# Moving the second batch's layer norm from cycles 1 to 5 into cycles 4 and 5 of the first batch's attention

## The reference

```python
x = L0_attn_x                                   # (8, 512, 256) float32
x = x + attn(_layernorm(x), gamma, w_qkv, w_out)
x = x + ffn(_layernorm(x), router_w, w1, b1, w2, b2)

def _layernorm(x, axis=-1, eps=1e-05):
    m = jnp.mean(x, axis=axis, keepdims=True)
    v = jnp.var(x, axis=axis, keepdims=True)
    return (x - m) / jnp.sqrt(v + eps)

xn = rms_norm(x, gamma); qkv = xn @ w_qkv       # inside attn
sim = einsum('bhid,bhjd->bhij', q * 64 ** -0.5, k)
out = einsum('bhij,bhjd->bhid', softmax(sim), v)  @ w_out
```

## Time and profile before

| | |
|---|---|
| median of 3 runs | 1148.58 us |
| lowest, highest | 1147.79, 1149.24 us |
| the profiled execution | 1149.06 us, of which its span is 1147.3 us |
| TensorE busy | 1132.5 us (99%) |
| VectorE busy | 1010.4 us (88%) |
| ScalarE busy | 859.6 us (75%) |
| GpSimd busy | 671.2 us (59%) |

### The profile page before, as it was taken

One profiled execution on the slowest core, in us unless ns is written; L12 is line 12 of the kernel. 1 busy time (PEld: TensorE's weight loads), 2 busy tenths in 40 slices (PEclk: granted clock), 3 DMA queues, 4 the chain that ended last, 5 costly groups with the idle time before them and its releaser, 6 DMA issues.

```text
span 1147.3 us, 29822 instructions
## 1 busy us (share of the span) xinstructions
PE 1132.5 (99%) x11664; PEld 959.6 (84%) x11664; DVE 1010.4 (88%) x1768; ACT 859.6 (75%) x1899; POOL 671.2 (59%) x827
## 2 busy tenths in 40 slices
PE   8999999999999999999999999999999999999998
PEld 6778888888888888888888888888888877888887
DVE  6899899889988998999898988898989988989975
ACT  6878888888888888888888888888888885334432
POOL 6776656565656565656565666666656576223421
PEclk9999999999999999999999999999999999999999
DMA  4134112311231123212221222122312235335321
GB/s 124 51 88 112 39 38 75 93 39 38 75 93 38 39 75 85 46 39 74 63 70 38 66 61 66 35 74 57 75 39 56 75 94 152 131 118 150 105 76 38
DMA packets 58284, 83.15 MB, mean 72 GB/s; under 512 B 12576, under 2 KB 34592, under 8 KB 58144
## 3 DMA queue, kind: packets, MB, share of 16 engines
q1 hardware_dynamic: 58144, 81.24, 26.1%
HBM read 31.14 MB, written 16.25 MB: 41 GB/s over the span
## 4 chain that ended last, share of the span: by engine, by line
PE 88%; DVE 8%; ACT 1%; issue 1%; POOL 1%; DMA 0%; SPq 0%; ACTq 0%; DVEq 0%; POOLq 0%
PE ps L659 22%; PE ps L777 19%; PE ps L809 14%; PE ps L697 10%; PE ps L742 10%; PE ps L703 5%; PE ps L952 3%; DVE pT_lo L1398 3%; PE ps L956 2%; DVE negmax L1485 1%; DVE f_o L1675 1%; PE ps L755 1%; ACT prob L1114 1%; DVE xT_lo L1399 1%; PE ps L957 1%
## 5 line engine op out<-in xcount | busy, mean ns | idle before, releaser
L1245 POOL TENSOR_SCALAR prob<-prob,rowinv 128x512 f32<-128x512 f32 x512 | 358.4, 716 | 323.6 <-DVE rowinv L1490 321.7
L1114 ACT ACTIVATE prob<-ps,negmax 128x512 f32<-128x512 f32 x512 | 349.2, 696 | 75.4 <-DVE negmax L1485 75.4
L1485 DVE TENSOR_REDUCE negmax<-ps 128x2 f32<-128x1024 f32 x256 | 311.6, 1218 | 56.5 <-PE ps L703 56.1
L1398 DVE TENSOR_TENSOR pT_lo<-ps,pT_hi 128x512 fp32r<-128x512 f32 (+1 forms) x384 | 319.0, 858 | 35.0 <-ACT pT_hi L1107 20.8
L742 PEld LDWEIGHTS ps<-identity,prob 64*128 64x128 f32 x4096 | 167.0, 139 | 40.0 <-DVE pT_lo L1398 5.9
L742 PE MATMUL ps<-identity,prob 64*128 64x64 f32 x4096 | 169.1, 222 | 2.8 <-DVE pT_lo L1398 2.0
L697 PE MATMUL ps<-nat 64*128 64x512 f32 x1024 | 166.1, 402 | 4.3 <-DVE nat L1398 2.4
L809 PE MATMUL ps<-xT_hi,wbig 64*128 64x512 f32 x992 | 159.1, 398 | 0.0
L1104 ACT ACTIVATE pT_hi<-ps 128x1024 fp32r<-128x1024 f32 x128 | 131.5, 1028 | 32.3 <-issue 23.7
L777 PE MATMUL ps<-pT_hi,vbuf 64*128 64x512 f32 x992 | 145.4, 411 | 0.0
L1107 ACT ACTIVATE pT_hi<-ps 128x512 fp32r<-128x512 f32 x256 | 140.2, 608 | 0.6 <-PE ps L742 0.5
(11 more groups left out here) (118 smaller groups left out, 2008.4 us busy)
## 6 DMA issues: line engine op xcount, KB each, us to landing
att_hi_v<-halves_out SPq DMA_DIRECT2D x128, 128.0 KB, 2.3
att_lo_v<-halves_out SPq DMA_DIRECT2D x128, 128.0 KB, 2.4
blocks_scratch<-xblocks SPq DMA_DIRECT2D x15, 512.0 KB, 3.0
xn<-blocks_scratch SPq DMA_DIRECT2D x60, 128.0 KB, 2.8
xin<-in_x SPq DMA_DIRECT2D x32, 128.0 KB, 3.2
xres<-in_x SPq DMA_DIRECT2D x8, 512.0 KB, 3.5
x_scratch<-xres SPq DMA_DIRECT2D x8, 512.0 KB, 2.6
xin<-x_scratch SPq DMA_DIRECT2D x32, 128.0 KB, 3.3
```

Source lines behind the costliest of these rows:

```text
L1114: act.activation(prob[:, n % NPROB, j * SEQ:(j + 1) * SEQ], ps[:, score_banks(n) + j, :], ACT.Exp, bias=negmax[:, n % 4, j:j + 1], accum_o ...
L1245: return pool.tensor_scalar(dst, src, scalar, 1.0, ALU.mult, ALU.mult)
L1398: return dve.tensor_tensor(dst, full, hi, ALU.subtract)
L1485: dve.tensor_reduce(negmax[:, n % 4, :], ps[:, score_banks(n):score_banks(n) + 2, :], AX.X, ALU.max, negate=True).then_inc(s_max, 1)
```

## The change

For the first batch alone another table is used. The four statistics steps stand in slots 16 to 19, which is cycle 4 (two in each half of the cycle), the normalisation of four tiles in slots 20 and 21 and the two block transposes in slots 22 and 23, which is cycle 5. Step 10 is left out for this batch, where it did nothing. The other batches keep their table.

```diff
 LN_SLOTS = {5: 0, 7: 1, 9: 2, 11: 3, 13: 10, 15: 6, 17: 8, 19: 9, 21: 13}
+FIRST_LN_SLOTS = {16: 0, 17: 1, 18: 2, 19: 3, 20: 6, 21: 8, 22: 9, 23: 13}
 LAST_LN_SLOT = NUNIT
...
             b, rel = divmod(slot, SPB)
-            return (b + 1, LN_SLOTS[rel]) if rel in LN_SLOTS and 0 <= b < B else None
+            places = LN_SLOTS if b else FIRST_LN_SLOTS
+            return (b + 1, places[rel]) if rel in places and 0 <= b < B else None
```

## The result

The changed kernel takes 1151.72 us (median of 8 runs, 1150.81 to 1153.53); eight runs of the kernel before have a median of 1149.11 us. The ratio is 1.0026, 95% interval 1.0017 to 1.0034: slower by about 0.26%, beyond what the measurement leaves open. (A ratio is worked out from all the runs of both kernels, so it can lie a few hundredths of a per cent off that of the two medians, here 1.0023.) The forecast was 1150.1 us and no change that can be told; it is wrong in both. The median lies 0.02 us above the top of the forecast's range. The profiled execution took 1150.88 us with a span of 1149.1, +1.8 us on that of before.

The account below looks back on a forecast made before the run. TensorE, busy 99% of the span, was taken to bound the kernel. -0.52 - 1.03 + 3.05 = +1.50 us on the profiled 1149.06 gave 1150.6, or 1150.1 on the median's scale; range 1147.7 to 1151.7.

Parts of the forecast that it names:

- Cycles 1 to 3: Statistics steps and normalisations removed from these cycles shorten them by 0.52 us together, bounds -0.3 and -0.75.
- Cycle 4: Normalisations leave, statistics come in; both TensorE waits go and the cycle becomes 14.95 us, -1.03.
- rival 3: Cycle 4: statistics are blocked too, beside GpSimd's split of chunk 6; +2.9 in sum, 1151.5 us; chance 0.06.
- the 1.30 us of the second half's steps: Cycle 4, ahead of tile 18's row maximum: two statistics, the aggregation and the variance take 1.30 us.
- Cycle 5: Four normalisations meet GpSimd's split of chunk 7; one stands until the split's low part ends; the cycle loses 3.05 us.
- rival 1: Cycle 5: normalisations run back to back and GpSimd's split is held up; -0.70 in sum, 1147.9 us; chance 0.12.
- rival 4: Cycle 5 has room for the moved steps and keeps its length; -1.55 in sum, 1147.0 us; chance 0.05.
- a stall at part speed: Cycle 5: VectorE and GpSimd share the port at part speed; four normalisations take 4.3 us, kernel near 1150.8.
- the wait for the exponential: Cycle 5: TensorE waits 0.7 us for an exponential, besides some 2 us for the low part of tile 18.
- rival 2: Cycle 5: TensorE's clock falls to 1.2 GHz behind its 2.0 us pause, costing 3.06 us; chance 0.07.
- The anchor: Base of the sum: profiled 1149.06 us lies 0.48 above the three-run median 1148.58, so 1150.6 becomes 1150.1.

Follow-up runs that it names:

- Experiment 2: Changed kernel with GpSimd's split of weight chunk 7 moved four slots later, from cycle 5 to cycle 6: 1148.43 us, ratio 0.9992.
- the second measurement: The changed kernel run again without an edit: 1151.65 us (11 runs), ratio 1.0024 against the kernel before.
- experiment 3: Changed kernel with 14 unneeded matmuls ahead of the queries and keys of pair 6, filling TensorE's pause in cycle 5: 1152.05 us, ratio 1.0026.
- filled kernels: 14 unneeded matmuls added to the changed kernel in cycle 5 (1152.05 us), or to the kernel before in cycle 5 (1151.65) or cycle 16 (1150.45).
- experiment 7: Changed kernel with another first-batch table, first normalisations in slot 15, the others in slot 19: 1147.97 us; with first two statistics in slots 7 and 8, 1147.99.
- 8-step kernels: Kernel before with 8 extra statistics steps in each of four cycles (1157.87 us), or in cycle 16 alone with a 192-byte (1152.96) or 1024-byte buffer (1151.37).

## Why the prediction was wrong

- **Cycles 1 to 3**: right, -0.58 for -0.52.
- **Cycle 4**: right in its mechanism, -0.89 for -1.03. Both waits went, the statistics were not blocked (rival 3 falls). The mis-sized term is the 1.30 us of the second half's steps: they took 1.47, because the variance, a small tensor-by-scalar instruction, took 0.39 us. The forecast had used cycle 2, where it took 0.19 and had begun in the same moment as GpSimd's multiplication (45.42). In cycle 4 it began 0.33 us into one and ended with it.
- **Cycle 5**: right, +3.03 for +3.05, with the place, the instruction that stands (2562 ns) and the instruction that makes it stand. GpSimd was not held up (rival 1 falls), there was no room (rival 4 falls), and a stall at part speed would have put the low part at +6.3, where it came at +5.57. Experiment 2 shows GpSimd's split as the cause. That the wait for the exponential was 0.48 us and not 0.7 cost nothing in the sum, which did not use it.
- **The step that failed is rival 2, TensorE's clock, which the sum had at nothing.** I saw the 2.0 us pause, gave the fall 0.07 and left it out of the range, with the words "no pause in this trace brought it about; none was that long". That the trace held no such pause was a lack of evidence, and I counted it as evidence against. The runs showed a lower clock in 15 of 19 executions of the changed kernel, and in none of 81 of before or of 11 with the pause gone (experiment 2). It cost 1.3 us where a profile caught it. The 3.06 of the rival was too much: a stretch of 3.4 us at half the clock can cost at most its half, 1.7 us, and the block behind the pause took 1.48 more, not its own length once more. As a term of the sum the clock is 15/19 x 1.3 = +1.0 by this estimate: 1.56 + 1.0 = +2.6. The medians gave +2.61 and, in the second measurement, +2.30; the ratios +3.0 and +2.8.
- **The anchor.** I took off 0.48 us to come from the profiled execution to the median of three runs. The kernel before measured 1149.11, 1149.35, 1149.32, 1148.45 and 1149.64 in the sets of runs since: that median had been a low one, and the 1149.06 of the profiled execution was the better base. Of the 1.62 us between forecast and result (1151.72 - 1150.1) this makes 0.53, the clock about 1.0 and the cycles 0.06. With the clock and without this step the sum gives 1149.06 + 2.6 = 1151.7.
- **Chance in it.** The result lies 0.02 us outside the range; the second measurement, 1151.65, would have lain 0.05 inside. Which side it fell on is chance. The miss isn't: the forecast's own spread ended at 1151.3, and what stretched the range to 1151.7 were rivals 1 and 3, of which neither came true.
- **What stays open.** The mean clock of each run shows how often it falls, and one profile of the changed kernel shows place and price, but no experiment removed the falls and nothing else: experiment 3 removed them and kept its time, and experiment 2 shortened the cycle too. The 1.0 us is therefore worked out, not isolated: by the runs of the changed kernel with and without a full clock it would be 0.9 x 15/19 = 0.7, and those with a full clock still lie 1.8 to 2.0 us above before instead of 1.56. Why filled kernels may take longer than their cycles, and why the feed-forward block sometimes loses up to 3 us, was not settled.

## What to carry to other kernels

When an edit makes the critical engine wait longer than any wait in the trace, the clock is a term of the sum, at the share of executions in which it may fall, and not a rival: a profile that happens to show a full clock doesn't say otherwise, the mean granted clock of all runs does. Before moving tensor-by-scalar work of VectorE, lay it beside GpSimd's long instructions: two normalisations moved away from the split gained 1.37 us here (experiment 7), without an instruction less. And compare cycle lengths, not just medians of three, when the terms are below a microsecond.

## What the runs showed of the hardware

- **A pause of 1.1 us can bring TensorE's clock down.** In the 8-step kernels 4 of 20 runs have a mean clock below 1.000: 2 of 4 with four such pauses, 1 of 5 and 1 of 11 with one. A pause of 1.15 us that the kernel before has at 941 us never did, in 81 runs. Each fall that a profile shows, three in three kernels, lasts 3.4 us at 1.2 GHz and costs 1.3 to 1.5 us.
- **An unused buffer of 192 bytes cost 0.20%** (0.11 to 0.29), one of 1024 bytes nothing that can be told. By the length of the cycles alone, 192 (14.633 us) and 1056 bytes (14.64) cost something and 768 and 1024 (14.607, as before) nothing. They differ in where the buffers behind them begin; which buffer matters was not tried, and 1056 bytes was tried only together with four pauses.
- **Other forms stop too.** Where the feed-forward block starts, a VectorE instruction with two inputs in SBUF (a subtraction, 1024 columns) and one of GpSimd (an addition, 512) meet: in before VectorE's starts first (969.76) and takes 1.23 us, GpSimd's (969.82) 2.32; in experiment 3 GpSimd's starts first (970.87) and takes 1.28, VectorE's (971.01) 2.23. Each time the one that starts second takes 1.0 us longer than the same instruction where it starts first (2.32 for 1.28, 2.23 for 1.23). A 128x4 tensor-by-scalar instruction took 0.39 us (74.72 to 75.11) when it began inside a multiplication of GpSimd that ran from 74.39 to 75.08, and 0.19 when both began at 45.42.
